# A fused four-layer kernel: the input of 22 tiles of the last layer is turned by the DMA instead of the matmul engine

## The chip, the cores and the metric

The kernel runs on one core of one Trainium2 chip. Its time is device microseconds of that core, the median of three runs. The profile is of one further execution.

## The reference

Four post-norm layers are applied to x of 4 x 1024 tokens by 1024 features, all in float32. Cut to what is computed:

```python
x = layernorm(x + x @ (weight * block_mask).T)                    # first dense layer
x = layernorm(x + x @ W1.T + bias + lora(x))                      # second dense layer
x = layernorm(x + state_space_and_mlp(x))                         # four small blocks of width 128, and a readout to 1024
x = layernorm(x + x @ W.T + b                                     # third dense layer
                + sum_e routing[batch, e] * (x @ A[e].T) @ B[e].T * 2)
# routing = softmax of router(mean of x over tokens 179 to 1022 of the batch)
```

## The kernel before, in words

Tokens are worked in 32 tiles of 128 tokens. Tile `s` is numbered through the three dense layers: 0 to 31 the first, 32 to 63 the second (`A_END` = 32), 64 to 95 the third (`B_END` = 64, `D_END` = 96); `TPB` = 8 tiles are a batch. A dense layer keeps its weights on the chip, in two walls, as a high and a low part, so that a product is three matmuls (`hi·hi`, `hi·lo`, `lo·hi`, lines 884 to 886): 16 chunks, 48 matmuls of 512 columns a tile. The lower-rank terms are added into the weights, so each batch of the second and third layers has walls of its own, built while the batch before runs (`build_parts`). Between the second and the third dense layer stands the state space part with the MLPs; its last piece, the readout (`read_out(c)`, lines 1154 to 1156), is spread over the steps of the third layer: readout tile `c` gives the input tile of the third layer, 8 tiles ahead of its use.

The order on each engine is written out by hand, one Python function for each engine, and held together by semaphores. SyncE (SP) issues the loads, ScalarE (ACT) and SyncE issue stores and loads in program order: a wait holds all that stands behind it on that engine. A step of the third layer, for tile `s` with `j = s % 8`, is:

- PE: `turn_x(s + 1)` turns the next input tile by 8 transposes of 128 x 128 into PSUM (line 896); then the 48 matmuls of tile s; in steps j = 0 to 3 of batches 1 and 2 (2 to 4 of batch 0) a readout of 6 matmuls after each half. `read_out(c)` waits until VectorE has taken readout `c - 1` out of the same banks (`c_added`). In step 4 `reduce_total` follows, the sum over tokens for the router of the next batch.
- ACT: `split_x(s + 1)` (the high part, line 1369), `normalise(s - 1)` and its store, then for the two readout tiles of the step before `normalise_c` (lines 1549 and 1552) and its store to `x3` (line 1556), then the high parts of the next weights where they are due.
- VectorE (DVE): the second half of tile s - 1, `split_x(s + 1)` (the low part, line 1823), `residual` of the second readout tile (lines 2230 to 2242), `add_up`, then the first half of tile s.
- SP: `load_x(s + 3)`, `load_z`, `load_c` (the residual input of a readout tile, line 681), the weights. `load_c` waits until the slot is stored (`c_stored`), three slots in turn.

In the second layer the input comes another way: GpSimd (POOL) parts the normalised float32 row of a tile into a plane of low and a plane of high 16 bits (`part_planes`), ACT stores them, SP loads each plane by a transposing DMA (line 632), and POOL joins the planes into `x_in` (`join_planes`, line 2640). There `turn_y` is something else: it turns the layer's output.

Of the kernel before, what the change touches and what calls it, by code (L numbers as in the profile page):

```python
# [5 lines left out]
P = 128  # L6
# [41 lines left out]
EARLY = 4  # L48

# [89 lines left out]
def x_loads(s):  # L139

    if s < A_END:
        return (s - FIRST) // 2 + 1
    even, odd = x_loads(A_END - 2), x_loads(A_END - 1)
    if s < B_END:
        return even + 2 * (s - A_END + 1)
    return (odd if s % 2 else even + 2 * TILES) + (s - B_END) // 2 + 1
# [10 lines left out]
def turn_count(s):  # L157
    return 2 * (s - A_END + 1) if s < B_END else 2 * TILES + s - B_END + 1
# [84 lines left out]
def build(nc, a, out):  # L243
# [5 lines left out]
    x3 = scratch("x3_scratch", (TILES, P, D))  # L249
# [133 lines left out]
    bias_rows = at("bias_rows", R, [P, D])  # L383
    cz = at("cz", R + 24576, [P, 2, 2, P], F32R)
# [43 lines left out]
    with ExitStack() as ctx:  # L428
# [175 lines left out]
        def _(sp):  # L604
# [4 lines left out]
            def load_x(s):  # L609
                if s >= D_END:  # L610
                    return

                if s - 2 >= B_END:
                    sp.wait_ge(x_turned, turn_count(s - 2))
                elif s == B_END + 1:
                    sp.wait_ge(lo_ready, split_count(B_END - 1))
                elif s > A_END:
                    sp.wait_ge(x_turned, turn_count(s - 1))
                elif paired(s - 2):
                    p = pair_of(s - 2)  # L620
                    last = A12 if s - 2 == S_BEG + 2 * p else A22
                    sp.wait_ge(hi_ready, op_count(p, last))
                    sp.wait_ge(lo_ready, op_count(p, last))
                    sp.wait_ge(x_summed, x_sums(p, SUMS - 1))
                elif s - 2 >= FIRST:
                    sp.wait_ge(hi_ready, split_count(s - 2))
                    sp.wait_ge(lo_ready, split_count(s - 2))
                if A_END <= s < B_END:
                    i = s - A_END
                    sp.wait_ge(stored[i % 2], 16 * (i // 2 + 1))  # L630
                    for part in range(2):
                        sp.dma_start_transpose(x_planes[:, part], x1[i, part]).then_inc(x_loaded[0], 16)
                elif s >= B_END:
                    c = s - B_END
                    if s == B_END + 1:
                        sp.wait_ge(y_rotated[0], MLP_END)
                        sp.wait_ge(y_rotated[1], MLP_END)
                    sp.wait_ge(c_stored[c_slot(c)], 16 * c_uses(c))
                    sp.dma_start(x_in[s % 2][:], x3[c]).then_inc(x_loaded[s % 2], 16)
                else:  # L640
                    sp.dma_start(x_in[s % 2][:], a["x_t"][s]).then_inc(x_loaded[s % 2], 16)
# [86 lines left out]
            for s in range(2, A_END):  # L728
# [11 lines left out]
                if s == S_END:  # L740
# [4 lines left out]
                    load_x(s + 3)  # L745
                if s > S_END:
# [6 lines left out]
                if s + 2 >= A_END:  # L753
                    load_x(s + 2)
# [46 lines left out]
            for b in range(BATCHES):  # L801
# [14 lines left out]
                for s in range(p + 2 if b == 0 else p, p + TPB):  # L816
                    j = s % TPB
                    load_x(s + 3)
# [19 lines left out]
        def _(pe):  # L838
# [470 lines left out]
            for b in range(BATCHES):  # L1309
# [36 lines left out]
        def _(act):  # L1346
# [4 lines left out]
            def split_x(s):  # L1351
# [6 lines left out]
                else:  # L1358
                    act.wait_ge(x_turned, turn_count(s))
                    src = x_in[1][:] if s < B_END else ps_x  # L1360
# [184 lines left out]
            def normalise_c(c):  # L1545
# [8 lines left out]
                act.wait_ge(c_normed, c + 1)  # L1554
                at_least(act, c_stored[c_slot(c)], 16 * (c_uses(c) - 1))
                act.dma_start(x3[c], place).then_inc(c_stored[c_slot(c)], 16)
# [58 lines left out]
            t_hi(7)  # L1615
            send_planes(3)
            split_x(FIRST + 3)
            normalise(4)
            evacuate(5, 0)
            for j in range(A11, S1):  # L1620
                op_hi(0, j)
            send_planes(4)
            evacuate(5, 1)
# [6 lines left out]
            for p in range(PAIRS):  # L1630
# [7 lines left out]
                if p > 0:  # L1638
                    send_planes(a - 2)
                normalise(a - 1)  # L1640
# [4 lines left out]
                hold(p, 1)  # L1645
# [36 lines left out]
            for s in range(A_END, B_END):  # L1682
# [18 lines left out]
                if s == A_END:  # L1701
                    send_planes(s - 1)
                if s > B_END - EARLY:
                    silu_x(s - 1 - B_END + EARLY)
                if s >= B_END - EARLY:
                    square1(s - B_END + EARLY)
# [35 lines left out]
            for b in range(BATCHES):  # L1742
# [11 lines left out]
                for s in range(p + 2 if b == 0 else p, p + TPB):  # L1754
# [4 lines left out]
                    for i in C_STEP[b].get(j - 1, ()):  # L1759
                        normalise_c(c + i)  # L1760
# [3 lines left out]
                    build_parts(n + PARTS, PART_STEP[b].get(j, ()))  # L1764
            normalise(D_END - 1)
# [4 lines left out]
        def _(dve):  # L1770
# [42 lines left out]
            def split_x(s):  # L1813
                src = x_first[:, s] if s < FIRST else x_in[s % 2 if s < A_END else 1][:] if s < B_END else ps_x
# [435 lines left out]
            def add_up(c, half):  # L2250
# [4 lines left out]
                dve.wait_ge(c_normed, c + 1)  # L2255
# [203 lines left out]
            for s in range(A_END, B_END):  # L2459
# [149 lines left out]
        def _(pool):  # L2609
# [68 lines left out]
            def root_c(c):  # L2678
                i = c % 2
                pool.wait_ge(c_ve_ready, 2 * c + 1)  # L2680
                at_least(pool, c_normed, c - 1)
# [3 lines left out]
            def add_up(c):  # L2685
# [4 lines left out]
                pool.wait_ge(c_normed, c + 1)  # L2690
# [58 lines left out]
            for s in range(S_END, A_END):  # L2749
                for i, n in enumerate(TAIL_PARTS[s]):  # L2750
# [5 lines left out]
                if s + 2 >= A_END:  # L2756
                    join_planes(s + 2)
# [3 lines left out]
            part_planes(A_END - 1)  # L2761
            for s in range(A_END, B_END):
                if s + 2 < B_END:
                    join_planes(s + 2)
                root(s)
                if B_END - EARLY <= s + 1 < B_END:
# [89 lines left out]
```

## Time and profile before

| | us |
|---|---|
| median of 3 runs | 1662.61 (1660.96 to 1665.57) |
| the profiled execution, its own time | 1665.42 |
| its span, first to last instruction | 1663.4 |
| PE busy in it | 1617.6 |
| DVE, ACT, POOL busy in it | 1171.7, 667.3, 615.5 |

The stages, in us from the span's start: the first dense layer to about 345, the second to about 800, the small blocks to about 1165, the third dense layer to the end. A row of a timeline has the start, the length, the engine, the line, the operation and its tiles; what stands in brackets at its end is how long the engine was idle before it, and what ended that.

### The profile page before, as it was taken

The page shows a single profiled execution, that of the slowest core. Times are in us where ns is not written, and L with a number is a line of the kernel's source. Part 1 is how long each engine was busy: PE and PEld are TensorE (multiplying, and loading weights), DVE is VectorE, ACT ScalarE, POOL GpSimd, SP SyncE. Part 2 cuts the span into 40 slices and gives each one's busy share as a digit, 9 for nine tenths or more (in the row PEclk, how much of TensorE's full clock was granted, in tenths as well). Part 3 has the DMA queues.
Part 4 walks back from the last instruction along what each step waited for, and adds up shares of the span by engine and source line. Part 5 has one row for each costly group of instructions (what it writes and reads, how often), then busy time and mean ns, then how long its engine had stood idle before and what let it go on. Part 6 is the DMA issues. An engine that isn't in the chain of part 4 may idle for free.

```text
span 1663.4 us, 22807 instructions
## 1 busy us (share of the span) xinstructions
PE 1617.6 (97%) x7734; PEld 1298.9 (78%) x7734; DVE 1171.7 (70%) x2150; ACT 667.3 (40%) x987; POOL 615.5 (37%) x507
## 2 busy tenths in 40 slices
PE   9999999999999999998899999999899999999998
PEld 7877777878888888887776676666688788888886
DVE  7878887646656565675777777778867777776633
ACT  3544444433333333322345555545533333333311
POOL 4324333443333222221477777772213212221200
PEclk9999999999999999999989999999999999999999
DMA  7233333544545444632140000002546555555421
GB/s 279 84 113 121 114 101 127 170 114 132 126 111 125 113 122 116 162 92 76 42 161 26 1 1 1 1 13 95 206 146 214 192 198 190 187 195 188 134 82 51
DMA packets 140195, 196.58 MB, mean 118 GB/s; under 512 B 75954, under 2 KB 84146, under 8 KB 139826
## 3 DMA queue, kind: packets, MB, share of 16 engines
q1 hardware_dynamic: 115250, 125.92, 25.9%
q10 hardware_dynamic: 24832, 69.22, 10.8%
q8 instruction: 63, 1.03, 0.3%
q14 instruction: 50, 0.41, 0.1%
HBM read 105.97 MB, written 72.35 MB: 107 GB/s over the span
## 4 chain that ended last, share of the span: by engine, by line
PE 75%; DVE 10%; issue 7%; POOL 3%; ACT 3%; DMA 2%; ACTq 0%; SPq 0%; POOLq 0%; DVEq 0%
PE ps L884 14%; PE ps L886 13%; PE ps L885 13%; PE ps L1130 6%; PE ps L1072 3%; PE ps L963 2%; PE ps L965 2%; PE ps L964 2%; PE ps L1030 2%; PE ps L1120 2%; PE ps L1078 2%; PE ps L1122 2%; PE ps L1121 2%; PE ps L896 2%; PE ps L1098 1%
## 5 line engine op out<-in xcount | busy, mean ns | idle before, releaser
L2622 POOL TENSOR_TENSOR rstd<-var_eps,minus_half 128x1 f32<-128x1 f32 x96 | 87.5, 911 | 562.1 <-DVE minus_mean L1908 561.9
L884 PE MATMUL ps<-wall_x,x_hi 128*128 128x512 f32 x688 | 277.0, 403 | 8.9 <-ACT wall_x L1475 3.1
L885 PE MATMUL ps<-wall_x,x_hi 128*128 128x512 f32 x688 | 271.4, 394 | 0.0
L886 PE MATMUL ps<-wall_x,x_lo 128*128 128x512 f32 x688 | 270.9, 394 | 0.0
L884 PE MATMUL ps<-wall_y,x_hi 128*128 128x512 f32 x512 | 201.9, 394 | 0.0
L885 PE MATMUL ps<-wall_y,x_hi 128*128 128x512 f32 x512 | 199.4, 389 | 0.0
L886 PE MATMUL ps<-wall_y,x_lo 128*128 128x512 f32 x512 | 199.4, 389 | 0.0
L884 PEld LDWEIGHTS ps<-wall_x,x_hi 128*128 128x128 f32 x688 | 131.1, 191 | 39.7 <-issue 5.4
L886 PEld LDWEIGHTS ps<-wall_x,x_lo 128*128 128x128 f32 x688 | 131.2, 191 | 28.6
L885 PEld LDWEIGHTS ps<-wall_x,x_hi 128*128 128x128 f32 x688 | 131.3, 191 | 25.6
L1840 DVE TENSOR_TENSOR row<-ps,bias 128x512 f32<-128x512 f32 x128 | 87.8, 686 | 86.7 <-PE ps L886 85.4
L1541 ACT ACTIVATE g<-ps,b 128x512 f32<-128x512 f32 x128 | 83.9, 679 | 123.8 <-PE ps L1122 123.4
L1130 PE MATMUL ps<-g,w 128*128 128x512 f32 x256 | 126.9, 619 | 0.0
L1843 DVE BATCH_NORM_STATS2 stats<-row 128x6 f32<-128x512 f32 x152 | 105.1, 694 | 28.8 <-ACT row L1403 24.3
L1410 ACT ACTIVATE shift<-minus_mean,rstd 128x1 f32<-128x1 f32 x96 | 28.0, 292 | 239.5 <-POOL rstd L2622 239.5
L1413 ACT ACTIVATE row<-row,shift,rstd 128x1024 f32<-128x1024 f32 x96 | 119.5, 1245 | 3.2
L886 PEld LDWEIGHTS ps<-wall_y,x_lo 128*128 128x128 f32 x512 | 96.1, 188 | 20.4
L885 PEld LDWEIGHTS ps<-wall_y,x_hi 128*128 128x128 f32 x512 | 96.2, 188 | 18.9
L884 PEld LDWEIGHTS ps<-wall_y,x_hi 128*128 128x128 f32 x512 | 96.2, 188 | 18.8
L2640 POOL COPY x_in<-x_planes 128x1024 uint16<-128x1024 uint16 x64 | 85.2, 1378 | 26.8 <-DMA x_planes<-x_scratch 26.8
L1369 ACT ACTIVATE x_hi<-ps 128x1024 fp32r<-128x1024 f32 x32 | 32.7, 1023 | 150.6 <-PE ps L896 147.6
L1072 PEld LDWEIGHTS ps<-mean_col,squares 128*128 128x128 f32 x520 | 68.1, 194 | 26.2 <-issue 12.0
(329 smaller groups left out, 3619.2 us busy)
## 6 DMA issues: line engine op xcount, KB each, us to landing
x_scratch<-row ACTq DMA_DIRECT2D x32, 512.0 KB, 2.7
x_in<-x_scratch SPq DMA_DIRECT2D x32, 512.0 KB, 3.9
out<-row ACTq DMA_DIRECT2D x32, 512.0 KB, 2.7
x_in<-in_x_t SPq DMA_DIRECT2D x29, 512.0 KB, 3.5
w_first<-in_w_t SPq DMA_DIRECT2D x56, 256.0 KB, 3.0
x_scratch<-planes_early ACTq DMA_DIRECT2D x27, 512.0 KB, 3.1
cx<-x_scratch SPq DMA_DIRECT2D x24, 512.0 KB, 4.2
x_scratch<-cx ACTq DMA_DIRECT2D x24, 512.0 KB, 3.6
```

Of the source, the lines that this page charges most:

```text
L884: pe.matmul(bank, hi[:, k], wall[:, k, 0, cols], start=(k == 0), stop=False)
L885: pe.matmul(bank, hi[:, k], wall[:, k, 1, cols], start=False, stop=False)
L886: return pe.matmul(bank, lo[:, k], wall[:, k, 0, cols], start=False, stop=(k == KC - 1))
L896: last = pe.transpose(ps_x[:, k * P:(k + 1) * P], x_in[s % 2][:, k * P:(k + 1) * P], ident[:])
L1072: last = pe.matmul(ps[:, bank, c:c + 1], squares[:, c * P:(c + 1) * P], mean_col[:], start=True, stop=True)
L1130: pe.matmul(ps[:, OUT], w2[:, FCH * (n // UNITS) + i], g[:, i], start=(i == 0), stop=(i == FCH - 1)).then_inc(o_done, 1)
L1413: act.activation(row[:, i], row[:, i], ACT.Identity, bias=shift[:, i:i + 1], scale=rstd[:, i:i + 1])\
L1541: act.activation(g[:, i], ps[:, F0 + i % 2], ACT.Silu, bias=of_layer(b1[:, :, i], n))\
L1840: dve.tensor_tensor(row[:, i, cols], ps[:, out_bank(s, half)], bias[:, cols], ALU.add)\
L1843: mark(dve.bn_stats(stats[:, i, half], row[:, i, cols]))
L2622: pool.tensor_tensor(rstd[:, i:i + 1], var_eps[:, i:i + 1], minus_half[:, 0:1], ALU.pow)\
L2640: pool.tensor_copy(halves[:, part], x_planes[:, part].rearrange("p k t -> p (k t)"))\
```

## The change

In the third layer, tiles 10 to 31 (`PLANES_FROM` = `B_END` + 10 and on) are no longer turned by PE. ACT parts the normalised readout tile into two planes of 16 bits (`part_c`: two copies of 128 x 1024 into one buffer `c_planes`, and a store), SP loads them by two transposing DMAs into the one buffer `x_planes` instead of one plain load, and ACT joins them into `x_in[1]` (`join_planes`, two more copies), from where `split_x` reads. The load moves from three tiles ahead to two. Besides, six pieces of order are changed: ACT holds the second block of a pair (`hold(p, 1)`) ahead of `normalise(a - 1)` in the first layer; ACT takes `split_x(6)` and `evacuate(5, 1)` ahead of a store; the load and the join of the second layer's first tile come earlier; the other joins of that layer are issued a step sooner in the text (which puts them ahead of `root1`); ACT squares ahead of the silu at the end of that layer; and DVE prepares tables (`prepare`) ahead of `split_y` there.

```diff
+C_PLANES = TPB + 2
+PLANES_FROM = B_END + C_PLANES
@@ load_x
+                if s > PLANES_FROM:
+                    sp.wait_ge(x_turned, turn_count(s - 1))
...
                     sp.wait_ge(c_stored[c_slot(c)], 16 * c_uses(c))
+                    if s >= PLANES_FROM:
+                        for part in range(2):
+                            sp.dma_start_transpose(x_planes[:, part], x3_planes[c - C_PLANES, part])\
+                              .then_inc(x_loaded[0], 16)
+                        return
@@ PE, third layer
-                    if s + 1 < D_END:
+                    if s + 1 < PLANES_FROM:
                         turn_x(s + 1)
@@ ACT
+            def part_c(c):
+                act.wait_ge(c_normed, c_norm_count(c))
                 at_least(act, c_stored[c_slot(c)], 16 * (c_uses(c) - 1))
+                if c > C_PLANES:
+                    act.wait_ge(c_stored[c_slot(c - 1)], 16 * c_uses(c - 1))
+                halves = c_place(c).bitcast(U16).rearrange("p (f h) -> p h f", h=2)
+                for part in range(2):
+                    act.activation(c_planes[:, part], halves[:, part], ACT.Identity).then_inc(c_normed, 1)
+                act.wait_ge(c_normed, c_norm_count(c) + 2)
+                act.dma_start(x3_planes[c - C_PLANES].rearrange("h p f -> p h f"), c_planes[:])\
+                   .then_inc(c_stored[c_slot(c)], 16)
+
+            def join_planes(s):
+                act.wait_ge(x_loaded[0], 16 * x_loads(s))
+                act.wait_ge(lo_ready, split_count(s - 1))
...
+                for part in range(2):
+                    act.activation(halves[:, part], x_planes[:, part].rearrange("p k t -> p (k t)"), ACT.Identity)\
+                       .then_inc(x_turned, 1)
@@ ACT, first layer
+                hold(p, 1)
                 normalise(a - 1)
...
-                hold(p, 1)
@@ ACT, third layer
-                    for i in C_STEP[b].get(j - 1, ()):
-                        normalise_c(c + i)
+                    late = C_STEP[b].get(j - 1, ())
+                    if late:
+                        normalise_c(c + late[0])
+                        part_c(c + late[0])
+                        normalise_c(c + late[1])
...
                     build_parts(n + PARTS, PART_STEP[b].get(j, ()))
+                    if PLANES_FROM <= s + 2 < D_END:
+                        join_planes(s + 2)
+                    if late:
+                        part_c(c + late[1])
@@ DVE, second layer
+                if b + 1 == BATCHES and j >= 3:
+                    prepare(j)
                 if i >= 1:
                     split_y(s - 1)
-                if b + 1 == BATCHES:
+                if b + 1 == BATCHES and j < 3:
                     prepare(j)
@@ POOL, second layer
-                if s + 2 < B_END:
-                    join_planes(s + 2)
                 root(s)
+                if s + 3 < B_END:
+                    join_planes(s + 3)
```

ACT's row in step j = 2 of batch 1 reads as follows, before. `c_shift` and `cx` are the normalisation of a readout tile.

```order
L1369 ACTIVATE x_hi<-ps 128x1024 [waits mm_done,x_turned]
L1410 ACTIVATE shift<-minus_mean,rstd 128x1 [waits rstd_ready,ve_ready]
L1413 ACTIVATE row<-row,shift,rstd 128x1024 [waits shift_ready]
L1417 DMA out<-row 128x1024 [waits normed]
L1549 ACTIVATE c_shift<-c_minus_mean,c_rstd 128x1 [waits c_rstd_ready,c_ve_ready]
L1552 ACTIVATE cx_147<-cx_147,c_shift,c_rstd 128x1024 [waits c_shift_ready]
L1556 DMA x_scratch<-cx_147 128x1024 [waits c_stored2,c_normed]
L1549 ACTIVATE c_shift<-c_minus_mean,c_rstd 128x1 [waits c_rstd_ready,c_ve_ready]
L1552 ACTIVATE cx_145<-cx_145,c_shift,c_rstd 128x1024 [waits c_shift_ready]
L1556 DMA x_scratch<-cx_145 128x1024 [waits c_stored0,c_normed]
```

And after, the same step from the end of its first normalisation (the names `x_planes` of the DMA rows stand for the scratch in HBM):

```order
L1578 ACTIVATE cx_147<-cx_147,c_shift,c_rstd 128x1024 [waits c_shift_ready]
L1592 ACTIVATE c_planes<-cx_147 128x1024 [waits c_stored1,c_stored2,c_normed]
L1592 ACTIVATE c_planes<-cx_147 128x1024
L1594 DMA x_planes<-c_planes 128x2x1024 [waits c_normed]
L1575 ACTIVATE c_shift<-c_minus_mean,c_rstd 128x1 [waits c_rstd_ready,c_ve_ready]
L1578 ACTIVATE cx_145<-cx_145,c_shift,c_rstd 128x1024 [waits c_shift_ready]
L1604 ACTIVATE x_in_126<-x_planes 128x1024 [waits lo_ready,x_loaded0]
L1604 ACTIVATE x_in_126<-x_planes 128x1024
L1592 ACTIVATE c_planes<-cx_145 128x1024 [waits c_stored2,c_stored0,c_normed]
L1592 ACTIVATE c_planes<-cx_145 128x1024
L1594 DMA x_planes<-c_planes 128x2x1024 [waits c_normed]
L1395 ACTIVATE x_hi<-x_in_126 128x1024 [waits mm_done,x_turned]
```

Six copies stand in the step where none stood, and the join, which waits for a load, stands ahead of the second parting and of the next step's `x_hi`.

SP's row from step j = 1 into step j = 2 of batch 1, after (`cz` is the readout's input; `cx` its residual input):

```order
L658 DMA_TRANSPOSE x_planes<-x_planes 128x8x128 [waits c_stored0,x_turned]
L658 DMA_TRANSPOSE x_planes<-x_planes 128x8x128
L713 DMA cz<-z_hi_scratch 128x128 [waits c_mm,zf_stored1]
L713 DMA cz<-z_lo_scratch 128x128
L713 DMA cz<-z_hi_scratch 128x128 [waits c_mm,zf_stored1]
L713 DMA cz<-z_lo_scratch 128x128
L703 DMA cx_146<-x_scratch 128x1024 [waits totalled1,totalled0,stored0,c_stored1,cx_loaded1]
L703 DMA cx_147<-x_scratch 128x1024 [waits totalled1,totalled0,stored1,c_stored2,cx_loaded2]
L658 DMA_TRANSPOSE x_planes<-x_planes 128x8x128 [waits c_stored1,x_turned]
L658 DMA_TRANSPOSE x_planes<-x_planes 128x8x128
```

The place of the loads of x among the other loads is the one they had; before, a plain load for a tile one further ahead stood there.

## Rows read from the trace of the kernel before

**Rows 1.** The page, part 1: busy us, share of the span, instructions.

```profile
PE 1617.6 (97%) x7734; PEld 1298.9 (78%) x7734; DVE 1171.7 (70%) x2150; ACT 667.3 (40%) x987; POOL 615.5 (37%) x507
```

**Rows 2.** Waits of PE: engine, line, waited for; us in total, times, longest.

```profile
PE ps L1072 <- ACT squares L1502: 6.0, 3, 2.8
PE ps L963 <- ACT held L1390: 5.1, 5, 1.6
PE ps L979 <- DVE w_first L1932: 3.9, 2, 3.2
PE ps L884 <- DVE row L1840: 3.0, 4, 2.1
```

**Rows 3.** Stretches: length, PE, PEld, DVE, ACT, POOL busy, PEclk, DMA, GB/s.

```profile
786.00:790.00 4.00, 4.00 (x14) 3.14 (x13) 2.63 (x5) 1.02 (x1) 0.00 (x0) 0.57 0.05 19
1353.80:1368.30 14.50, 14.50 (x69) 12.09 (x68) 12.04 (x25) 5.53 (x7) 4.64 (x5) 1.00 0.69 238
```

**Rows 4.** Timeline of PE, steps of batch 1, third layer: start, length, instruction.

```profile
1339.33 1.03 PE L896 MATMUL ps<-ident,x_in 128*128 128x128 f32 x8
...
1340.67 0.39 PE L886 MATMUL ps<-wall_y,x_lo 128*128 128x512 f32 x1
...
1353.59 0.40 PE L1156 MATMUL ps<-wout_hi,cz 128*128 128x512 f32 x1
1353.83 1.03 PE L896 MATMUL ps<-ident,x_in 128*128 128x128 f32 x8
...
1382.83 1.03 PE L896 MATMUL ps<-ident,x_in 128*128 128x128 f32 x8
1394.61 1.84 PE L1164 MATMUL ps<-token_weight,total 128*128 128x1 f32 x16
1396.31 1.07 PE L896 MATMUL ps<-ident,x_in 128*128 128x128 f32 x8
```

**Rows 5.** Timeline of ACT, step j = 2 of batch 1.

```profile
1354.90 1.03 ACT L1369 ACTIVATE x_hi<-ps 128x1024 fp32r<-128x1024 f32 x1 [6.84 <-PE ps L896]
...
1358.19 1.24 ACT L1552 ACTIVATE cx<-cx,c_shift,c_rstd 128x1024 f32<-128x1024 f32 x1
1359.46 0.33 ACTq L1556 DMA_DIRECT2D x_scratch<-cx  x1
1361.85 0.29 ACT L1549 ACTIVATE c_shift<-c_minus_mean,c_rstd 128x1 f32<-128x1 f32 x1 [2.42 <-POOL c_rstd L2682]
```

**Rows 6.** Timeline of SP, the same step.

```profile
1356.12 6.35 SPq L681 DMA_DIRECT2D cx<-x_scratch  x2
1362.57 0.38 SPq L639 DMA_DIRECT2D x_in<-x_scratch  x1
```

**Rows 7.** Timeline of DVE and PE, the same step.

```profile
1355.96 1.23 DVE L1823 TENSOR_TENSOR x_lo<-ps,x_hi 128x1024 fp32r<-128x1024 f32 x1 [1.39 <-ACT x_hi L1369]
...
1358.42 0.67 DVE L2230 TENSOR_TENSOR cx<-ps,cx 128x512 f32<-128x512 f32 x1
...
1360.16 0.39 PE L1154 MATMUL ps<-wout_hi,cz 128*128 128x512 f32 x1
```

**Rows 8.** Timeline of SP and POOL, second layer: transposing loads and their joins.

```profile
387.54 2.59 SPq L632 DMA_TRANSPOSE x_planes<-x_scratch  x2
392.62 2.66 POOL L2640 COPY x_in<-x_planes 128x1024 uint16<-128x1024 uint16 x2 [0.77 <-DMA x_planes<-x_scratch]
...
415.13 2.73 SPq L632 DMA_TRANSPOSE x_planes<-x_scratch  x2
...
421.57 3.05 POOL L2640 COPY x_in<-x_planes 128x1024 uint16<-128x1024 uint16 x2 [2.13 <-DMA x_planes<-x_scratch]
```

**Rows 9.** Groups of ACT: instructions, busy us, mean ns, idle before.

```profile
L1369 ACT ACTIVATE x_hi<-x_in 128x1024 fp32r<-128x1024 f32 x41 | 43.4, 1059 | 27.6 <-POOL x_in L2640 23.3 <-POOL planes_early L2633 3.6 <-POOL planes_late L2633 0.6
L1383 ACT ACTIVATE x_hi<-x_in 128x512 fp32r<-128x512 f32 x30 | 18.4, 617 | 0.0
```

More of the change, by code:

```diff
@@ L157, in turn_count, with by_dma, c_norm_count @@
 def turn_count(s):
-    return 2 * (s - A_END + 1) if s < B_END else 2 * TILES + s - B_END + 1
+    return 2 * (s - A_END + 1) if s < B_END else 2 * TILES + s - B_END + 1 + max(0, s - PLANES_FROM + 1)
+def by_dma(s):
+    return A_END <= s < B_END or s >= PLANES_FROM
+def c_norm_count(c):
+    return c + 1 + 2 * max(0, c - C_PLANES)
 def before_in_slot(s):
@@ L248, in build @@
     x2 = scratch("x2_scratch", (TILES, P, D))
-    x3 = scratch("x3_scratch", (TILES, P, D))
+    x3 = scratch("x3_scratch", (C_PLANES, P, D))
+    x3_planes = scratch("x3_planes", (TILES - C_PLANES, 2, P, D), U16)
     h0 = scratch("h0_scratch", (P, TOKENS))
@@ L383, in build @@
     bias_rows = at("bias_rows", R, [P, D])
+    c_planes = at("c_planes", R + 20480, [P, 2, D], U16)
     cz = at("cz", R + 24576, [P, 2, 2, P], F32R)
@@ L745, in _ @@
                     load_x(s + 3)
+                if s + 2 == A_END:
+                    load_x(A_END)
                 if s > S_END:
@@ L817, in _ @@
                     j = s % TPB
-                    load_x(s + 3)
+                    if s + 3 < PLANES_FROM:
+                        load_x(s + 3)
+                    if s + 2 >= PLANES_FROM:
+                        load_x(s + 2)
                     for i in Z_LOAD[b].get(j, ()):
@@ L1359, in split_x @@
                     act.wait_ge(x_turned, turn_count(s))
-                    src = x_in[1][:] if s < B_END else ps_x
+                    src = x_in[1][:] if by_dma(s) else ps_x
                 if s == B_END:
@@ L1615, in _ @@
             t_hi(7)
+            split_x(FIRST + 3)
             send_planes(3)
-            split_x(FIRST + 3)
             normalise(4)
@@ L1621, in _ @@
                 op_hi(0, j)
+            evacuate(5, 1)
             send_planes(4)
-            evacuate(5, 1)
             normalise(5)
@@ L1702, in _ @@
                     send_planes(s - 1)
+                if s >= B_END - EARLY:
+                    square1(s - B_END + EARLY)
                 if s > B_END - EARLY:
                     silu_x(s - 1 - B_END + EARLY)
-                if s >= B_END - EARLY:
-                    square1(s - B_END + EARLY)
                 if i >= 1:
@@ L1813, in split_x @@
             def split_x(s):
-                src = x_first[:, s] if s < FIRST else x_in[s % 2 if s < A_END else 1][:] if s < B_END else ps_x
+                src = x_first[:, s] if s < FIRST else x_in[s % 2 if s < A_END else 1][:] if s < A_END or by_dma(s) else ps_x
                 hi, lo = [flat(t) for t in x_parts(s)]
@@ L2254, in add_up @@
                     return
-                dve.wait_ge(c_normed, c + 1)
+                dve.wait_ge(c_normed, c_norm_count(c))
                 if i == 1:
@@ L2680, in root_c @@
                 pool.wait_ge(c_ve_ready, 2 * c + 1)
-                at_least(pool, c_normed, c - 1)
+                if c >= 2:
+                    pool.wait_ge(c_normed, c_norm_count(c - 2))
                 pool.tensor_tensor(c_rstd[:, i:i + 1], c_var_eps[:, i:i + 1], minus_half[:, 0:1], ALU.pow)\
@@ L2689, in add_up @@
                     return
-                pool.wait_ge(c_normed, c + 1)
+                pool.wait_ge(c_normed, c_norm_count(c))
                 if i == 1:
@@ L2749, in _ @@
             for s in range(S_END, A_END):
+                if s + 2 == A_END:
+                    join_planes(A_END)
                 for i, n in enumerate(TAIL_PARTS[s]):
```

20 lines of the change are left out of this document (13 added, 7 removed).

## The prediction

> **What bounds the kernel now.** I read the page first: PE is busy 97% of the span and no other engine more than 70% [rows 1], so only what PE is spared, or made to wait for, moves the end. Next the waits of PE, to see what it lacks before the change [rows 2]: nothing of the third dense layer is among the four largest. Then the stretches: a whole step of the third layer runs at clock 1.00 with PE busy all 14.50 us [rows 3], and ACT has 5.53 us of work in it. Last the timelines of one such step, engine by engine, to see how far from late each wait stands. The reader should see that PE has no gap there, and that ACT and SP work by chains with little to spare.
>
> **What PE is spared.** A step lasts 14.50 us (1339.33 to 1353.83), and 57 matmuls from 1340.67 to 1353.59 stand 0.227 us apart [rows 4]. Of the step 60 x 0.227 = 13.60 us are matmuls, so turning a tile costs 0.90 us of PE, not the 1.03 its row shows. Twenty-two tiles give 22 x 0.90 = 19.8 us, if nothing else comes late.
>
> **What the other order of the first two layers gives.** The held blocks: 5.1 us of waits [rows 2] that end with a copy standing behind a normalisation. I take 4. The start of the second layer: one wait of 3.2 us, within the 3.9 [rows 2], on a weight part that DVE takes late, because it sat waiting for ACT's split, and this for POOL's join; the load now goes out ahead of weights and the join is free sooner. I take 3. The end of that layer: the squares' waits, the larger two of 6.0 us, and the row's 2.1 [rows 2]; the clock fell to its lower level of 1.2 GHz behind the first (0.57 granted in 786 to 790) [rows 3], which costs (1 - 0.57) x 4 = 1.7 us each. The table work moves ahead of a wait for PE's transposes, and the joins ahead of `root1`. Of 2.8 + 2.0 + 2.1 + 2 x 1.7 = 10.3 I take 8. Sum 15; the bounds are 4 and 19. What could be late next is the normalisation behind a held block, by the 0.6 us of the copy; it has slack of its own in POOL's waiting.
>
> **What ACT is given.** Each tile has two copies for the parting and two for the join, 128 x 1024 of 16 bits. No row shows such a copy on ACT. Bounds: 0.62 us, the price of 512 elements [rows 9], if 16 bits were to go twice as fast, and 1.36, what the join costs POOL (half of 2.66 and a bit) [rows 8]. I take 1.03 to 1.06, as for 1024 elements [rows 5, 9], and for a pair, whose ends overlap, 1.95. In steps without readouts this hides in ACT's 9 us of idleness: 3.9 of some 10.9 us. In the readout steps of batch 0 only the parting is new, in gaps of ACT. There I charge nothing; uncovered, it would be 1 to 2 us a batch. In the readout steps of batches 1 and 2 it doesn't hide, because ACT now waits in the step for SP.
>
> *The loop.* Count from A, the start of `x_hi` in a step. The first readout tile is normalised at A + 4.53 (1358.19 + 1.24 - 1354.90) [rows 5]. Parting ends at 6.5, the store goes at 6.55 and has landed 2.7 later: SP, waiting for the store sent at 1359.46, went on at about 1362.15, one load of `cx` (0.4) ahead of the x load at 1362.57 [rows 5, 6]. So `cx` goes at 9.25 and the transposing loads at 9.7: they stand behind that `load_c` in SP's row, as the x load did. From the issue of the pair to the join POOL needed 5.1 and 6.4 us [rows 8]; they were behind a load of 256 KB there, and here it is 512 KB. I take 5.7. So ACT's join can start at A + 15.4. Meanwhile ACT has normalised the second tile (A + 7.0 to 8.5, as now at 1361.85 [rows 5]) and stands idle for some 7 us, with the next split behind the join. The join ends at 17.35, the second parting at 19.3, its store is issued by 19.8. **A step of ACT takes 19.8 us against 13.6 of PE's.** Three steps, j = 1, 2 and 3, wait so; in step 4 the transposing load waits for no `load_c`. On SP the pair costs 2.59 us [rows 8] where the plain load cost 0.38 [rows 6]; behind it stand `cz` loads for readouts of the next step, some 10 us away, which hide the 2.2 us; uncovered, they would lengthen the same waits by as much. The DMA engines are 0.69 busy in such a step [rows 3], so I charge their share in the landing alone.
>
> *What PE waits for.* With T the start of PE's step, A is now T + 1.07. The low part starts at A + 1.06, the second half of the second readout's residual at A + 3.5 and ends at 4.2 (1358.42 is its first operation of the second half) [rows 7], and the readout that needs its banks comes at T + 6.33 (1360.16) [rows 4, 7]. There is slack of about 1 us for the first half. So as soon as A is more than some 2 us late, PE stops in its readout. Take T = 0 for step 1. The split needn't wait for PE's transposes any more, but the normalisation behind it waits for the statistics of the tile before, so I set A1 = 0.5. Then A2 = 20.3, A3 = 40.1, A4 = 59.9. PE stands in steps 2 and 3, which costs nothing beyond ACT's lateness. In step 4 `reduce_total` needs the last readout tile, normalised at A4 + 8.5 and added up by about A4 + 10.1: 70.0. It takes 1.7 (1394.61 to 1396.31) [rows 4], so step 5 starts at 71.7. Without the waits it would be 3 x 13.60 + (13.48 - 0.90) = 53.4 (13.48 from 1382.83 to 1396.31). **Delay 18.3 us in each batch.** PE idles 4 to 7 us at a time, and a wait of 2.8 us was followed by 4 us of 0.57 clock [rows 2, 3]; behind the last stop that adds 1.7. Two batches: 2 x 20.0 = 40.0 us. Behind step 4 ACT is back in time, since the next join finds its data.
>
> **A rule against the trace.** The landing of the pair is 5.1 to 6.4 us here [rows 8]. The Trainium skill, DMA: Bandwidth & Descriptors, section "Latency and other measured facts", gives transposing DMAs an effective 261 GB/s, by which the 512 KB of a tile would take an estimated 2.0 us. With 2.0 for 5.7 an ACT step is 16.1, a batch loses 7.2 + 1.7, and the sum would be 17 us below the time before. The trace does not agree, and I go by it. For a copy on ACT, which no row shows in 16 bits, the Trainium skill, ScalarE: Activation LUTs, section "What ACT_TABLE_LOAD costs", states 186 ns + 0.833 ns an element for float32 and bf16 alike, an estimated 1.04 us, which would leave the sum within a microsecond.
>
> **The sum.** - 19.8 - 15 + 40.0 = + 5.2 us. Against the profiled execution's own 1665.42 (span 1663.4) this is 1670.6. That execution lies 2.8 above the median of the runs, 1662.61, so as a median I predict 1668.
>
> **Rivals.**
> 1. *The same loop, but shorter.* Copies at 0.62 (a pair 1.15: three pairs save 2.4) and landing at 5.1 (0.6): an ACT step of 16.8, A4 = 50.9, step 5 at 62.7, 9.3 + 1.7 a batch, 22 in all: 22 - 34.8 = - 12.8, time 1650. For it: ACT's row is short where the element count is [rows 9]. Against it: the price goes by elements there, not by bytes.
> 2. *Faster: the join is never waited for.* If SP got past `load_c` early, or PE had more slack than rows 7 show, only what is spared is left: - 34.8, time 1628. Decides: whether A stays within 2 us of T in steps 2 and 3. Against it: SP's order, and the x load that went at 1362.57, 8.7 us into the step [rows 6].
> 3. *Slower: a longer loop.* Copies as slow as POOL's (a pair 2.6: 2.0 a step more) and landing at 6.4 (0.7): an ACT step of 22.5, A4 = 68.0, step 5 at 79.8, 26.4 + 1.7 a batch, 56 in all: + 21.4, time 1684. Decides from an ACT step of 20.5 up.
> 4. *The change of order gives 4 instead of 15*, because each wait removed is followed by the next: + 16, time 1679.
>
> **Chances.** The forecast 45% (its own range 1659 to 1678), rival 1 22%, rival 2 8%, rival 3 16%, rival 4 9%. A change of 0.3% (5 us) is about what a measurement can tell from none. The forecast lies at this bound: of its 45% I give 27 to slower, 15 to no change, 3 to faster. Rival 1 is faster but for 4, rival 2 faster, rival 3 slower, rival 4 slower but for 4. Faster 0.29, same 0.23, slower 0.48. The range reaches past rival 1 and rival 3, 1645 to 1688, and leaves out rival 2 and the ends.
>
> **What the profile after would show.** PE: 256 - 176 = 80 transposes of x, steps of 13.6 us where nothing waits. The loop right: in batches 1 and 2 ACT idle about 7 us before the join three times each, ended by the DMA of `x_planes`; three waits of PE each, at `read_out` and at `reduce_total`, on DVE's `cx` and on `total`, 3 to 7 us long, with lower clock behind them. Wrong: PE busy through those steps (rival 2), or ACT's 16-bit copies far from 1.05 us (rivals 1 and 3). The order right: the waits on `held`, on `w_first` and on the squares gone from PE's list. The forecast falls if the landing is near 2 us, or if the stores of the planes land much later than 2.7.

## The result, and the profile after

| | us |
|---|---|
| after, median of 4 runs | 1690.47 (1689.04 to 1693.32) |
| before, beside it, median of 4 runs | 1664.09 (1660.96 to 1666.62) |
| ratio | 1.0157, 95% interval 1.0132 to 1.0181 |
| the profiled execution after, its own time; its span | 1691.64; 1689.7 |

The change costs 26 us. I had predicted a loss of 5 (median 1668, range 1645 to 1688). The page after, part 1 (busy us, share of the span, instructions), stands against [rows 1]:

```profile
PE 1610.7 (95%) x7558; PEld 1289.0 (76%) x7558; DVE 1176.8 (70%) x2150; ACT 766.0 (45%) x1075; POOL 627.7 (37%) x507
```

PE has 176 matmuls less, which should spare 19.8 us, and is only 7 us less busy, in a span 26 us longer: part of what is left runs at the lower clock, as shown below. ACT has 99 us more work, the 88 copies. The waits of PE after (us in total, times, longest) stand against [rows 2]:

```profile
PE ps L1180 <- DVE cx L2286: 20.8, 4, 6.4
PE ps L1190 <- DVE total L2323: 13.0, 2, 7.4
PE ps L989 <- DVE row L1949: 12.6, 9, 2.3
PE ps L1012 <- DVE w_in L1988: 3.6, 4, 1.5
...
PE ps L1098 <- ACT squares L1545: 1.9, 2, 1.4
...
PE ps L1098 <- ACT squares L1528: 1.1, 1, 1.1
...
PE ps L1005 <- DVE w_first L1988: 0.7, 1, 0.7
```

The first two are the loop: two stops at the readout (`cx`) and one at the sum over tokens (`total`, the running sum that `reduce_total` needs), in each of batches 1 and 2. The third is new and in the first layer. The fourth, on `w_in` (a loaded part of the next batch's weights, to which DVE adds the lower-rank product), was 0.6 us before. The waits on `held` are gone, those on `w_first` and on the squares smaller.

To see where the time went I matched the same instruction of DVE in both timelines, tile by tile. After minus before, in us:

| place (DVE's start before / after) | after - before |
|---|---|
| first layer, start of the tail (298.39 / 308.49) | + 10.1 |
| second layer, from its fifth tile on (402.58 / 407.63) | + 5.1 |
| end of the second layer (798.06 / 789.03) | - 9.0 |
| third layer, batch 1, end of step j = 0 (1338.16 / 1328.74) | - 9.4 |
| end of step j = 5 (1409.45 / 1421.83) | + 12.4 |
| batch 2, step j = 0 (1457.02 / 1468.51) | + 11.5 |
| batch 2, step j = 5 (1528.32 / 1560.94) | + 32.6 |
| last tile (1656.09 / 1682.41) | + 26.3 |

The first layer loses 10.1, the second gains 19.1. In batch 1 the difference grows by 21.8 while five turns of 0.9 are spared: a loss of 26.3. In batch 2 it is 21.1 + 4.5 = 25.6. From there to the last tile 6.3 us are given back: nine spared turns, 8.1, less 1.8 at the new wait for `w_in`. So a turn gives back 0.9, as predicted.

One turn of the loop in ACT's timeline after, steps j = 2 and 3 of batch 1, against [rows 5] (start, length, instruction; in brackets the idle time before):

```profile
1352.47 1.06 ACT L1395 ACTIVATE x_hi<-x_in 128x1024 fp32r<-128x1024 f32 x1 [0.52 <-ACT c_planes L1592]
...
1357.35 2.00 ACT L1592 ACTIVATE c_planes<-cx 128x1024 uint16<-128x1024 uint16 x2
1359.38 0.38 ACTq L1594 DMA_DIRECT2D x_planes<-c_planes  x1
...
1368.59 2.57 ACT L1604 ACTIVATE x_in<-x_planes 128x1024 uint16<-128x1024 uint16 x2 [7.15 <-DMA x_planes<-x_planes]
1371.02 1.98 ACT L1592 ACTIVATE c_planes<-cx 128x1024 uint16<-128x1024 uint16 x2
1373.03 0.38 ACTq L1594 DMA_DIRECT2D x_planes<-c_planes  x1
1373.51 1.06 ACT L1395 ACTIVATE x_hi<-x_in 128x1024 fp32r<-128x1024 f32 x1 [0.51 <-ACT c_planes L1592]
```

And SP's, against [rows 6]:

```profile
1354.81 7.75 SPq L703 DMA_DIRECT2D cx<-x_scratch  x2
1362.66 3.00 SPq L658 DMA_TRANSPOSE x_planes<-x_planes  x2
```

The two `cx` loads stretch over 7.75 us because the second waits for ACT's store of 1359.38, and the transposing loads go out behind it at 1362.66. The join starts 5.93 us after that and ACT was idle for 7.15. The turn, from one `x_hi` to the next, lasts 21.04.

PE's timeline shows what a stop leaves behind, and the stretches (length, PE, PEld, DVE, ACT, POOL busy, PEclk, DMA, GB/s) the clock, against [rows 3, 4]:

```profile
1355.53 0.76 PE L1180 MATMUL ps<-wout_hi,cz 128*128 128x512 f32 x1 [6.44 <-DVE cx L2286]
...
1376.57 0.76 PE L1180 MATMUL ps<-wout_hi,cz 128*128 128x512 f32 x1 [4.58 <-DVE cx L2286]
...
1403.77 3.55 PE L1190 MATMUL ps<-token_weight,total 128*128 128x1 f32 x16 [5.61 <-DVE total L2323]
```

```profile
1356.00:1360.00 4.00, 4.00 (x11) 2.90 (x11) 3.86 (x9) 3.42 (x5) 2.24 (x2) 0.50 0.78 243
1404.00:1412.00 8.00, 8.00 (x27) 6.96 (x28) 2.73 (x7) 4.93 (x6) 0.55 (x1) 0.50 0.72 169
```

Behind each of the three stops PE runs at 0.50, its lower level of 1.2 GHz: the 16 matmuls of the sum over tokens take 3.55 us instead of 1.84.

### The profile page after: what moved, and what is told of

Its sections match the earlier page's. It is cut to its first block, busy times and chain, and to the rows that moved or that the text cites. A ratio compares the mean times of both kernels' runs of the same rounds, so it can differ in the third digit from the quotient of the medians.

```text
span 1689.7 us, 22567 instructions
## 1 busy us (share of the span) xinstructions
PE 1610.7 (95%) x7558; PEld 1289.0 (76%) x7558; DVE 1176.8 (70%) x2150; ACT 766.0 (45%) x1075; POOL 627.7 (37%) x507
## 4 chain that ended last, share of the span: by engine, by line
PE 68%; DVE 12%; ACT 7%; issue 7%; DMA 4%; POOL 2%; SPq 1%; ACTq 1%; DVEq 0%; POOLq 0%
PE ps L910 13%; PE ps L912 12%; PE ps L911 12%; PE ps L1156 6%; PE ps L1098 3%; PE ps L1056 2%; PE ps L1104 2%; ACT c_planes L1592 2%; PE ps L1146 2%; PE ps L1148 2%; PE ps L1147 2%; DMA x_planes<-x_planes 2%; PE ps L1124 1%; PE ps L989 1%; PE ps L991 1%
## 5 line engine op out<-in xcount | busy, mean ns | idle before, releaser
L2680 POOL TENSOR_TENSOR rstd<-var_eps,minus_half 128x1 f32<-128x1 f32 x96 | 97.6, 1017 | 549.3 <-DVE minus_mean L1964 549.3
L1879 DVE TENSOR_TENSOR x_lo<-x_in,x_hi 128x1024 fp32r<-128x1024 f32 x63 | 77.6, 1232 | 65.8 <-ACT x_hi L1395 65.4
L912 PEld LDWEIGHTS ps<-wall_y,x_lo 128*128 128x128 f32 x512 | 97.2, 190 | 20.7
L911 PEld LDWEIGHTS ps<-wall_y,x_hi 128*128 128x128 f32 x512 | 97.4, 190 | 19.8
L2691 POOL COPY planes_early<-row 128x1024 uint16<-128x1024 uint16 x54 | 67.0, 1270 | 62.6 <-ACT row L1439 46.6
```

What stands on the lines that cost most here:

```text
L911: pe.matmul(bank, hi[:, k], wall[:, k, 1, cols], start=False, stop=False)
L912: return pe.matmul(bank, lo[:, k], wall[:, k, 0, cols], start=False, stop=(k == KC - 1))
L1879: dve.tensor_tensor(lo, src, hi.bitcast(F32), ALU.subtract).then_inc(lo_ready, 1)
L2680: pool.tensor_tensor(rstd[:, i:i + 1], var_eps[:, i:i + 1], minus_half[:, 0:1], ALU.pow)\
L2691: pool.tensor_copy(planes[s >= S_END][:, part], halves[:, part]).then_inc(parted, 1)
```

## The experiments

All were timed over five rounds beside the kernel before. The ratios are to it.

| run | median us | ratio, 95% interval |
|---|---|---|
| third layer's change alone | 1700.39 | 1.0199 (1.0174 to 1.0224) |
| order changes alone | 1656.12 | 0.9936 (0.9920 to 0.9952) |
| held block ahead, alone | 1675.63 | 1.0052 (1.0036 to 1.0069) |
| after, held block undone | 1683.67 | 1.0098 (1.0080 to 1.0117) |
| start of second layer, alone | 1656.35 | 0.9943 (0.9926 to 0.9961) |
| end of second layer, alone | 1651.08 | 0.9916 (0.9897 to 0.9935) |
| after, load ahead | 1653.19 | 0.9914 (0.9891 to 0.9936) |
| the same, held block undone | 1642.74 | 0.9869 (0.9846 to 0.9891) |
| after, PE kept busy at five of the six stops | 1691.33 | 1.0154 (1.0135 to 1.0173) |
| after, last stop filled | 1690.23 | 1.0151 (1.0127 to 1.0175) |
| load ahead, held undone, both normalised first | 1654.21 | 0.9926 (0.9907 to 0.9944) |
| the same, weights first | 1656.48 | 0.9939 (0.9917 to 0.9961) |
| load ahead, held undone, weights first | 1641.10 | 0.9854 (0.9833 to 0.9875) |
| the same, last stop filled | 1638.97 | 0.9857 (0.9823 to 0.9891) |

### Which part costs

The third layer alone: all of the diff but the six pieces of order.

> The change of the third layer alone, the order of the first two layers as before. Theory (the terms are independent; read from the two traces, after minus before: first layer + 10.1 us, second layer - 19.2, third layer + 35.4 = - 19.8 spared + 55.2 of loop and clock): the time before + 35, about 1699. Rival (the first layers and the third share something, such as the clock's state or the phase in which the third layer is entered, so that the third layer costs less alone): under 1690. By the prediction's own terms it would have been the time before + 20, 1684.

The order changes alone:

> The order changes of the first two layers alone, the third layer as before. Theory (terms independent): + 10.1 - 19.2 = - 9 us, about 1655, PE waiting some nine times for DVE's joined row of the first layer. Prediction on record: - 15, 1649. Rival: the new waits of the first layer are chance of one execution and go: - 19, 1645.

Measured + 33 and - 11 us. Their sum, + 22, is near the + 26 of both together. The terms of my forecast gave + 20 for the third layer and - 15 for the order. Of the six pieces of order, five are taken up below; the sixth, `split_x(6)` and `evacuate(5, 1)` ahead of a store, was not run apart.

### The held block of the first layer

```diff
@@ ACT, first layer (on the kernel before)
+                hold(p, 1)
                 normalise(a - 1)
...
-                hold(p, 1)
```

> Only the held block of a pair ahead of the normalisation, in the first layer. Theory: the held copy waits for PE's product, and the normalisation, the next high parts, the sums and the join stand behind it; the chain comes back to PE as a wait for DVE's row at each pair: + 10 us, about 1674. Prediction on record: - 4 us, 1660. Rival: the loss of the first layer comes from the other swap at its start (a split and an evacuation ahead of a store), then this run is within 2 us of before.

The reverse edit, on the changed kernel:

> The changed kernel with that one swap of the held block undone. Theory: 10 us less than the changed kernel, about 1680, and the waits of PE for DVE's row of the first layer gone, those for the held block back. Rival (the other swap is the cause): about 1690, the waits for DVE's row still there.

Measured + 8.7 us (0.0052 of 1666.66) alone, and 1.0098 against 1.0157, some 10 us, back when undone (6.8 by the medians, whose kernels before differ by 2.6). With it undone PE's waits for DVE's row in the first layer are gone and those for `held`, 5.1 us, are back. PE's waits in the first run (us in total, times, longest):

```profile
PE ps L963 <- DVE row L1893: 12.1, 9, 2.3
```

The changed kernel's timelines of ACT, DVE and PE over one pair show the way round:

```profile
167.50 0.60 ACT L1416 ACTIVATE held<-ps 128x512 f32<-128x512 f32 x1 [3.99 <-PE ps L991]
167.99 0.28 ACT L1436 ACTIVATE shift<-minus_mean,rstd 128x1 f32<-128x1 f32 x1
168.31 1.24 ACT L1439 ACTIVATE row<-row,shift,rstd 128x1024 f32<-128x1024 f32 x1
169.46 0.61 ACT L1409 ACTIVATE x_hi<-x_in 128x512 fp32r<-128x512 f32 x1
```

```profile
170.10 0.69 DVE L1906 TENSOR_TENSOR x_lo<-x_in,x_hi 128x512 fp32r<-128x512 f32 x1 [2.65 <-ACT x_hi L1409]
...
176.02 0.68 DVE L1949 TENSOR_TENSOR row<-ps,held 128x512 f32<-128x512 f32 x1
```

```profile
156.32 0.47 PE L989 MATMUL ps<-wall_y,x_hi 128*128 128x512 f32 x1 [0.91 <-DVE row L1949]
...
176.84 0.47 PE L989 MATMUL ps<-wall_y,x_hi 128*128 128x512 f32 x1 [1.22 <-DVE row L1949]
```

ACT stands at the held block for 3.99 us because PE's product isn't done, and behind it stand the normalisation, whose data was ready (it has no wait of its own), and `x_hi`. DVE gets `x_hi` late, the four sums and the low parts follow, then the joined row, for which PE waits. The circle is 20.5 us. Before, the normalisation went ahead of this wait, and four pairs (127.68 to 205.67) took 19.5 each, the next three (to 267.63) 20.7. In the changed kernel eight pairs (112.71 to 282.38) took 21.2. Part of this is the clock: behind two of the nine waits, of 2.21 and 1.99 us, its mean was 0.92 over the 22 us of a pair (134 to 156, 260 to 282), where the kernel before has 1.00 in all of its pairs. That is an estimated 1.8 us each, 3.5 of the 10.1.

### The second layer

Start: the loads and joins earlier, and the joins ahead of `root1`. End: the squares ahead of the silu, the tables ahead of `split_y`.

> On the kernel before, only the earlier loads and joins of the second layer. Theory (read from the traces: the second layer's start gave 5.1 us, with the wait for the first weights gone): before - 5, 1660. Prediction on record for this piece: - 3. Rival (the gain at the start needs the first layer's delay): within 2 us of before, 1665.

> On the kernel before, only the squares ahead of the silu (ACT) and the tables ahead of split_y (DVE), at the end of the second layer. Theory (read from the traces: 14.1 us between the last dense tiles): before - 14, about 1651. Prediction on record for this piece: - 8, 1657. Rival (the joins ahead of root1 are what brings the end forward): - 5 or less.

Measured - 9.5 and - 14.0 us. In the first one's trace 5.6 are gained by the fifth tile and 3.9 more at the end of the layer, where `root1` stands behind the joins; that it is this which gives the 3.9 was not run apart. Both pieces gave more than my 3 and 8. Together they overlap: 19.1 in the changed kernel.

### Is it the loop, or ACT's work?

```diff
@@ SP, third layer (on the changed kernel)
-                    if s + 2 >= PLANES_FROM:
+                    if s + 2 >= PLANES_FROM and not C_LOAD[b].get(j - 1):
                         load_x(s + 2)
                     for i in Z_LOAD[b].get(j, ()):
                         load_z(c + i)
+                    if s + 3 >= PLANES_FROM and C_LOAD[b].get(j):
+                        load_x(s + 3)
                     for i in C_LOAD[b].get(j, ()):
                         load_c(c + i)
```

> The changed kernel, but in the readout steps SP issues the transposing loads of the next tile ahead of the cx loads that wait for ACT's store, instead of behind them. Theory (the loop ACT - store - SP's order - landing - ACT costs 55 us with the clock): the join finds its data, ACT's step is its own work alone, 21.0 - 7.2 of idleness = 13.9 us against PE's 13.6, and the third layer loses at most 1 us a step in three steps of two batches: 1690 - 55 + 2 to 6 = 1637 to 1641, PE's stops at the readout and at the sum over tokens gone, clock 1.00 there. Rival (ACT has too much to do, wherever the load stands): the copies, 6.6 us a step, stay in the chain and the time falls by less than 20 us, to over 1670.

Every copy is still there, and 37 to 40 us are gone (1690.47 to 1653.19; 1.0157 to 0.9914). ACT's timeline of that kernel:

```profile
1350.77 1.06 ACT L1397 ACTIVATE x_hi<-x_in 128x1024 fp32r<-128x1024 f32 x1 [0.52 <-ACT c_planes L1594]
...
1359.65 2.57 ACT L1606 ACTIVATE x_in<-x_planes 128x1024 uint16<-128x1024 uint16 x2
1362.09 1.98 ACT L1594 ACTIVATE c_planes<-cx 128x1024 uint16<-128x1024 uint16 x2
...
1364.60 1.06 ACT L1397 ACTIVATE x_hi<-x_in 128x1024 fp32r<-128x1024 f32 x1 [0.53 <-ACT c_planes L1594]
```

The join doesn't wait, ACT's step is 13.83 us against 13.6 of PE's, and PE has no stop at the readout left. The loop is shown. The gain is 12 to 13 us less than the 49 to 53 expected. In the profiled execution, the slowest of the six, two waits of PE for `total` are left, and the lower clock behind them:

```profile
1391.08 3.54 PE L1192 MATMUL ps<-token_weight,total 128*128 128x1 f32 x16 [3.44 <-DVE total L2325]
...
1511.40 2.06 PE L1192 MATMUL ps<-token_weight,total 128*128 128x1 f32 x16 [2.47 <-DVE total L2325]
```

The waits are 5.9 us. Behind them PE worked at 0.50 for 9.3 and 3.4 us, an estimated 6.3 lost: 12.2 in all, about what is missing.

> The same, with the held block of the first layer again behind the normalisation. Theory (terms independent): 9 to 10 us less than the kernel with the load ahead, about 1629, the fastest of all. Rival: above 1650.

With the held block undone too the time is 1642.74, 10 us less and the least so far, and 14 above what I expected. The reason just given holds here too: its two waits for `total` are 2.74 and 4.02 us.

### What is left of it

Both readout tiles normalised before the first is parted:

```diff
@@ ACT, third layer
                         normalise_c(c + late[0])
-                        part_c(c + late[0])
                         normalise_c(c + late[1])
+                        part_c(c + late[0])
```

> The kernel with the load ahead and the held block undone, and in addition ACT normalises both readout tiles of a step before it parts the first. Theory (what is left of the loss in batches 1 and 2 is the parting, 2.0 us and an issue, that stands ahead of the second normalisation and so of the sum over tokens): PE's waits for total, 2.7 and 4.0 us, fall under 1.5 each, and the lower clock behind them goes: 6 to 9 us less, about 1635. Rival (what is late there is ACT's step as a whole, 13.9 against 13.6 us): the waits stay, within 2 us of 1643.

This theory fell: some 10 us slower (0.9869 to 0.9926, or 1642.74 to 1654.21). PE's waits in it:

```profile
PE ps L1186 <- DVE cx L2292: 5.7, 9, 1.8
PE ps L1196 <- DVE total L2329: 5.4, 3, 2.2
```

ACT now waits 2.41 us for the second tile's statistics with nothing to do, where it parted the first before, so its step is 16.1 to 16.6 us long instead of 13.8, and small waits return at nine readouts. The parting had been filling a wait.

> The same, and in the steps in which weights are loaded the transposing loads go out behind two of the weight loads. Theory (PE's wait for w_in, 1.5 us in each of batches 1 and 2 since the change, comes from weight loads that stand behind the transposing loads): 3 us less than the kernel above, about 1632. Rival (the join then comes too late for the next split): slower than the kernel above by 3 us or more.

```diff
@@ SP, third layer: the load leaves the step's start where PART_STEP has parts
                         if i + 4 < PARTS:
                             load_w(n + PARTS + i + 4)
+                        if i % KC == 1 and s + 2 >= PLANES_FROM:
+                            load_x(s + 2)
```

> The kernel with the load ahead and the held block undone (the parting of the first tile again between the two normalisations), and the transposing loads behind two of the weight loads in the steps that load weights. Theory (as between the two kernels that normalised both first, where the trace after differed by 1.4 us): 1 to 3 us less, 1641 beside 1643, so within what can be measured. Rival: slower by 3 us or more, the join late for the split.

Neither order of the loads can be told from the other by the times: 1656.48 beside 1654.21, 1641.10 beside 1642.74. PE's waits for `w_in` stay at 3.6 in all, 1.50 of it in each batch, so this theory fell. The changed kernel's traces of ACT, DVE and PE show another chain:

```profile
1439.48 2.56 ACT L1604 ACTIVATE x_in<-x_planes 128x1024 uint16<-128x1024 uint16 x2
1442.08 1.06 ACT L1395 ACTIVATE x_hi<-x_in 128x1024 fp32r<-128x1024 f32 x1
1443.17 1.23 DVE L1879 TENSOR_TENSOR x_lo<-x_in,x_hi 128x1024 fp32r<-128x1024 f32 x1 [1.84 <-ACT x_hi L1395]
1444.31 0.68 DVE L1988 TENSOR_TENSOR w_in<-ps,w_in 128x512 f32<-128x512 f32 x1
1445.05 0.50 PE L1012 MATMUL ps<-b_hi,a_hi 128*128 128x512 f32 x1 [1.50 <-DVE w_in L1988]
```

The join starts without a wait, so its data was there, but its 2.56 us stand ahead of `x_hi`, which before the change began right behind ACT's last weight copy. DVE waits 1.84 us for `x_hi`, its addition to `w_in` stands behind `x_lo`, and PE waits 1.50 for that. The kernel with the weights first has the same chain with the same two waits. No run moved the join here, so this is read from the traces and not tested.

### The clock behind the stops

```diff
@@ PE, third layer (stay_busy: matmuls of 128x512 into an unused bank)
                         if tiles and k == KC - 1:
+                            if s > PLANES_FROM and half == 0:
+                                stay_busy({2: 24, 3: 28}.get(j, 0))
                             read_out(c + tiles[half])
                     if j == SUM_STEP[b]:
+                        if b > 0:
+                            stay_busy(24)
                         reduce_total(b + 1)
```

> The changed kernel, with matmuls of 128x512 into banks that nobody reads where PE stops: 24 and 28 ahead of the readouts of steps j = 2 and 3, 24 ahead of the sum over tokens, in batches 1 and 2 (some 5.4 and 6.3 us of work each at 0.227). They compute nothing. Theory (PE at 1.2 GHz behind each stop; only the last of the three is not hidden by the loop, 4.0 us in each batch): the granted clock stays near 1.00 there and the time falls by about 8 us, to 1682. Rival 1 (the slow PE is part of the loop): the first two stops count also, up to 20 us less, 1670. Rival 2 (the clock is without effect, or the matmuls overflow the gaps): the same or slower, 1690 to 1700.

The condition leaves out step j = 2 of batch 1, whose tile is `PLANES_FROM` itself, so three of the four readout stops were filled. The first stretch below lies behind one of them, and the clock stayed up. Before the sum 3.14 us of stop were left, and it fell all the same, as the second shows:

```profile
1376.00:1380.00 4.00, 4.00 (x19) 3.30 (x18) 3.86 (x9) 3.42 (x5) 2.25 (x2) 1.00 0.85 301
1404.00:1412.00 8.00, 8.00 (x27) 6.99 (x28) 2.78 (x7) 4.98 (x6) 0.55 (x1) 0.50 0.74 164
```

The time is unchanged. ACT's second and third turns in it are 21.0 and 21.5 us in batch 1 and 20.7 and 21.4 in batch 2, where the changed kernel has 21.0 and 20.0, 19.7 and 21.4. None became shorter by more than 0.1 us, so the slow PE behind the readout stops isn't part of the loop: ACT and SP set it. The last stop was still open, and the next run fills it alone, with `stay_busy(38)`:

> The changed kernel with 38 matmuls of 128x512 (8.6 us) into a bank that nobody reads ahead of the sum over tokens in batches 1 and 2, and none at the readouts: where 24 of them were followed by waits of 3.1 and 3.8 us and by the lower clock, this leaves waits under 1. They compute nothing. Theory (the clock behind the last stop costs 4.0 us a batch, of it 1.7 in the sum over tokens and the rest in the step behind it): the sum's 16 matmuls last 1.84 us instead of 3.55, and the time falls by 6 to 8 us, to 1683. Rival (that time is lost elsewhere, in a late split of the next step): 1690, though the clock stays up.

```profile
1403.62 1.84 PE L1194 MATMUL ps<-token_weight,total 128*128 128x1 f32 x16
...
1540.07 1.84 PE L1194 MATMUL ps<-token_weight,total 128*128 128x1 f32 x16
```

The sum takes 1.84 us, clock 1.00 in both stretches behind it. From step j = 4 to 5 this profile loses 1.5 and 2.8 us less than the changed kernel's, though the filling ran 2.6 and 1.6 us past the moment at which `total` was complete (1400.98, 1538.46). Added, the clock's part is 4.1 and 4.4 us. The changed kernel's clock agrees: from PE's restart on it was 0.50 for 8.3 and 9.5 us, of which half, an estimated 4.2 and 4.7, is lost. The median shows none of it (1.0151 against 1.0157): the overrun took 4.2 of the 8.5, and the four other executions had a mean clock of 0.980 to 0.982 where the profiled one had 0.986; in what stretch they lost it the runs don't show. So the 4 us are read from one execution and not confirmed by the times.

> The kernel with the load ahead, the held block undone and the weights first, with 10 matmuls (2.3 us) that compute nothing ahead of the sum over tokens in batches 1 and 2, whose waits were 2.7 and 4.0 us. Theory (a wait of 4.0 was followed by the lower clock and one of 2.7 not): the clock stays up behind both, 2 to 4 us less than without them. Rival: no change within 2 us.

1638.97, ratio 0.9857: the same as without the filling within the intervals. The theory rested on a wrong reading. Behind the wait of 2.74 us, in the kernel with the load ahead and the held block undone, the sum itself took only 1.92 us, but the clock fell right behind it, as the stretch shows:

```profile
1384.00:1388.00 4.00, 4.00 (x14) 3.18 (x14) 1.48 (x4) 3.39 (x5) 0.55 (x1) 0.57 0.74 116
```

With the filling the waits are 1.91 and 0.54 us. Behind the first the clock fell again, to 0.50 for about 3 us, and behind the second it stayed up.

It and the kernel without it (0.9854) beat both kernels, by 24 us against before and about 50 against after.

## Why the prediction was wrong, step by step

- **What PE is spared:** right. 0.9 us a tile, 19.8 in all.
- **The loop:** right as a mechanism, at the places named (ACT idle 7 us before the join, ended by the DMA; two stops at `read_out` and one at `reduce_total`, 4.4 to 7.4 us long), mis-sized. The term "ACT's step 19.8" measured 23.7, 21.0 and 20.0 in batch 1, and 22.7, 19.7 and 21.4 in batch 2. The parts of the second: the normalised tile at A + 4.9 (4.53 predicted), the transposing loads at A + 10.2 (9.7), the landing 5.9 (5.7), the join 2.43 (1.95), all short by a little. The first turn has 2.6 more, because its normalisation stood for 2.43 us at the statistics. I had set this at 0.5 by "A1". So the two batches lose 22 and 21 us by the loop (26.3 and 25.6 less 4.1 and 4.4 for the clock) where I had 18.3.
- **The clock:** I charged 1.7 behind the last stop, from a fall seen behind a wait of 2.8. It is 4.1 and 4.4 by the one trace that isolates it, which the times of that kernel don't confirm.
- **A term put at nothing:** in steps without readouts I let ACT's new copies hide in its idle time. In step j = 6 the join doesn't hide: it stands ahead of `x_hi`, and PE waits 1.5 us for `w_in` in each of batches 1 and 2, 1.8 with what is around it.
- **The held blocks:** wrong in sign. I took - 4 and wrote that the normalisation would be late by 0.6, the copy. It is late by the wait for PE in front of the copy, 4 us, and that wait closes a circle through DVE: + 10.1 in the trace, + 8.7 when run alone. This is the step that failed worst, 14 us.
- **The second layer:** right in sign, too small: - 19 for - 11. By luck this hides 8 us of the errors in the other direction.
- **The sum:** - 19.8 + 10.1 - 19.1 - 0.4 + 51.9 + 3.6 = + 26.3 where I had - 19.8 - 15 + 40 = + 5.2 (51.9 is the loop and the clock of both batches, 3.6 the waits for `w_in`, - 0.4 a drift between the end of the second layer and batch 1). The miss of 21.1 is 14.1 from the held blocks, 11.9 from the loop and its clock and 3.6 from `w_in`, less 8.1 from the second layer and 0.4 of drift. Rival 3 (a longer loop, 1684) named the direction; its copies as slow as POOL's hold for the join alone, and its landing of 6.4 us was 5.9.

The rule I had weighed against the trace gives too short a time for these loads too. The join starts 5.9 us after the pair's issue began, and SP's issuing alone lasts 3.0 of them. By the 261 GB/s (stated for a non-contiguous middle dimension) of the Trainium skill, DMA: Bandwidth & Descriptors, section "Latency and other measured facts", 512 KB would be an estimated 2.0 us. The two copies of a kind differ on ACT:

```profile
L1604 ACT ACTIVATE x_in<-x_planes 128x1024 uint16<-128x1024 uint16 x44 | 56.5, 1351 | 50.3 <-DMA x_planes<-x_planes 48.4 <-ACT row L1439 1.9
L1592 ACT ACTIVATE c_planes<-cx 128x1024 uint16<-128x1024 uint16 x44 | 43.9, 1045 | 2.9 <-DMA x_planes<-c_planes 2.5
```

The parting, 1045 ns, is the estimated 1.04 us of the Trainium skill, ScalarE: Activation LUTs, section "What ACT_TABLE_LOAD costs". The join, which writes every second 16 bits, took 1351 ns, 0.31 us more than that estimate.

## What to carry to other kernels

Before an instruction is moved ahead of another on an in-order engine, ask what the moved one waits for, not how long it runs: everything behind it now waits for that too, and if the chain comes back to the engine waited for, each round is lengthened. A load whose data is long ready can still be late because it stands in a queue behind one that waits for this step's work; look for the order in the queue before you give up a change that seems to need too much of an engine. Work that stands ahead of a wait may be filling it.

## What was not expected of the hardware

- Behind PE's stops of 4.4 to 7.4 us in the changed kernel the granted clock was 0.50 for 3 to 9.5 us after PE had restarted. Stops of 1.6 to 2.8 us before the sum over tokens were followed by it as well, in every kernel with the load ahead. Where the sum took 3.11 and 2.70 us (the weights first) the fall came during it; where it took 1.92 and 2.06 us it came at its end or just behind, for about 3 us. The length of a stop alone doesn't tell: in the first layer of the changed kernel one of 2.21 us was followed by 0.58 in the stretch 135 to 139, and one of 2.32 by 1.00 in 219 to 223.
- Executions of one kernel differ in their mean clock. The one with the load ahead took 1657.63 us at 0.984 and 1644.59 at 0.992: 0.008 of 1650 is an estimated 13.2 us, the whole difference. With the held block undone too it was 1651.14 at 0.986 and 1637.22 at 0.992, where the clock gives 9.9 of 13.9.
- A 16-bit copy of 1024 elements on ACT takes 1045 ns when it reads every second element and 1351 when it writes every second.
